# A convolved-attention stage: block-shaped matmuls of a step in one section, transposes, scores and projections in another

## What is computed

```python
    B, T, D = x.shape                       # 8, 256, 256
    hd = D // H                             # 16 heads of 16
    attn = jnp.einsum('bhqd,bhkd->bhqk', q, k) * hd ** (-0.5)
    ...                                     # kernels: 9 taps for each of the B*H maps, from the context
    attn0 = jnp.where(mask, 0.0, attn).reshape(1, B * H, T, T)
    attn = lax.conv_general_dilated(attn0, kernels, window_strides=(1, 1), padding=((1, 1), (1, 1)),
                                    feature_group_count=B * H, ...).reshape(B, H, T, T)
    attn = jnp.where(mask, -jnp.inf, attn)
    p = jax.nn.softmax(attn, axis=-1)
    out = jnp.einsum('bhqk,bhkd->bhqd', p, v)
```

## Time and profile before

| | |
|---|---|
| median of 3 runs | 2229.43 us (2223.65 to 2230.05) |
| the profiled execution | 2223.91 us, span 2222.2 us |
| mean granted clock of TensorE in it | 0.907 |
| the stage's regular part, 632 to 1022 us | 390.0 us, granted clock 1.00 |
| busy in that part: TensorE, ScalarE, VectorE, GpSimd | 337, 206, 204, 200 us |

### The profile page before, as it was taken

The page is one execution under the profiler, slowest core; times in us unless marked ns, Lnnn a source line. Parts: engine busy times, 40 slices in busy tenths (PEclk is TensorE's granted clock), DMA queues, the critical chain, the costliest instruction groups (busy, mean ns, idle before and its releaser), DMA issues. The chain is left out here.

```text
span 2222.2 us, 40660 instructions
## 1 busy us (share of the span) xinstructions
PE 1821.4 (82%) x13563; PEld 1308.2 (59%) x13585; DVE 1031.4 (46%) x3515; ACT 957.6 (43%) x2468; POOL 743.3 (33%) x904
## 2 busy tenths in 40 slices
PE   6849999989598888887499988984893988887594
PEld 5737766666344444444389965644782866555493
DVE  2552224653455555553400058865346546984323
ACT  3633221432345555555333346754442435775220
POOL 1012202110355555542011054410645737641233
PEclk9959999999699999999689999995895998999697
DMA  4313212000311111100289944416676685433394
GB/s 146 115 52 133 64 41 94 19 20 8 54 35 32 34 36 33 34 20 9 84 322 355 332 132 103 114 51 254 197 150 252 183 150 136 108 93 123 98 352 128
DMA packets 171224, 260.81 MB, mean 117 GB/s; under 512 B 23056, under 2 KB 136592, under 8 KB 166928
## 3 DMA queue, kind: packets, MB, share of 16 engines
q1 hardware_dynamic: 150960, 208.65, 28.9%
q0 software_dynamic: 16704, 45.64, 9.3%
q10 hardware_dynamic: 3360, 3.93, 0.7%
HBM read 181.46 MB, written 37.75 MB: 99 GB/s over the span
## 5 line engine op out<-in xcount | busy, mean ns | idle before, releaser
L508 POOL DMA_INDIRECT weights_xg<-xn_rows,token_of x197 | 189.2, 961 | 418.9 <-DVE token_of L698 168.5
L1893 ACT ACTIVATE heads_probsT<-heads_ps_e 128x512 f32<-128x512 f32 x256 | 148.1, 597 | 69.2 <-PE heads_ps_e L1736 62.4
L1047 PE MATMUL experts_ps_g<-weights_w,experts_xT 128*128 x504 | 136.4, 395 | 1.7 <-issue 0.7
L1070 PE MATMUL experts_ps_y<-weights_w,experts_hT 128*128 (+1 forms) x486 | 134.1, 385 | 1.2 <-DVE experts_y L1132 1.2
L2224 PE MATMUL heads_ps_t<-ident,heads_mixes 128*128 128x128 f32 x576 | 103.5, 288 | 32.0 <-ACT heads_probsT L2318 19.5
L2307 ACT ACTIVATE heads_mixes<-heads_mixes,heads_least 128x256 f32<-128x256 f32 x288 | 118.4, 497 | 17.9 <-DVE heads_least L2464 17.9
L1712 PE MATMUL heads_ps_m<-heads_stackK,heads_stackQ 96*128 96x256 bf16 x512 | 100.1, 280 | 23.6 <-DMA heads_stackQ<-heads_q_pieces 9.4
L1104 ACT ACTIVATE experts_silu<-experts_ps_g 128x128 f32<-128x128 f32 (+1 forms) x165 | 53.0, 321 | 153.2 <-PE experts_ps_u L1052 80.3
L2201 PE MATMUL heads_ps_c<-heads_S,heads_band 32*32 32x512 f32 x3072 | 112.8, 606 | 0.4 <-DVE heads_least L2464 0.4
L2318 ACT COPY heads_probsT<-heads_ps_t 128x240 f32<-128x240 f32 x256 | 84.8, 362 | 64.4 <-PE heads_ps_t L2224 62.7
L2224 PEld LDWEIGHTS heads_ps_t<-ident,heads_mixes 128*128 128x128 f32 x576 | 60.1, 141 | 79.3 <-issue 70.1
(11 more groups left out here) (443 smaller groups left out, 4319.3 us busy)
## 6 DMA issues: line engine op xcount, KB each, us to landing
experts_w<-in_experts_dram SPq DMA_DIRECT2D x23, 2180.0 KB, 10.4
weights_w<-in_experts_dram SPq DMA_DIRECT2D x32, 768.0 KB, 5.7
weights_w<-in_experts_dram SPq DMA_DIRECT2D x14, 1536.0 KB, 18.7
y_rows<-experts_y SPq DMA_DIRECT2D x125, 128.0 KB, 1.8
heads_stackK<-heads_k_pieces SPq DMA_DIRECT2D x192, 64.0 KB, 2.6
heads_stackQ<-heads_q_pieces SPq DMA_DIRECT2D x192, 64.0 KB, 3.1
weights_w<-in_experts_dram SPq DMA_DIRECT2D x8, 1088.0 KB, 5.5
xn_rows<-xn SPq DMA_DIRECT2D x4, 2048.0 KB, 7.6
```

The source lines that it names most:

```text
L508: pool.indirect_dma_start(self.xg[:, u, :], None, xn_dram, bass.IndirectOffsetOnAxis(ap=tb.token_of[:, j:j + 1], axis=0)).then_inc(self.x_ ...
L1047: last = pe.matmul(ps_g[:, j % 2, 0:2 * F], xT[:, j % 2, c, :], w[:, bass.ds(at_slot(at[j], c * 2 * F), 2 * F)], start=(c == 0), stop=(c = ...
L1070: last = pe.matmul(ps_y[:, j % BY, 0:D], hT[0:m, j % 2, f * P:(f + 1) * P], w[0:m, bass.ds(at_slot(at[j], DC * 2 * F + f * D), D)], start= ...
L1893: act.activation(probsT[:, h, :], ps_e[:, h % 2, :], ACT.Exp).then_inc(exped, 1)
```

## The change

Nothing that is computed changes, and no instruction is added or removed but waits. The orders on TensorE and VectorE change, with the banks and the semaphore counts that follow from them:

- TensorE's step begins with the three taps of the convolution in a row, then the mix, then score_last of quad n+1. These are all the products that use tiles smaller than the array's full width. Behind them the turns; convolve_last stands behind turn 1, the third score behind turn 3, the fourth behind turn 5, the query and key projection behind turn 5 (it was 2), the value projection behind turn 6 (it was 3). The first two scores, of quad n+2, end the step behind turn_back.
- The scores 0 and 2, score_last and the query projection use bank 0 of ps_s; the scores 1 and 3, convolve_last and the value projection bank 1. The ninth-strip score now comes third of its quad.
- ORDER puts the ninth strip fourth instead of first. VectorE interleaves: drops 0 and 1 of quad n+1, row_max 0 and 1, drop_masked_last, row_max 2 to 4, drop 2, row_max 5 and 6, drop 3, row_max 7 and 8, then finish and take as before.
- ScalarE places the values behind copy 7 (it was 4).

```diff
-    ORDER = (8, 0, 4, 1, 5, 2, 6, 3, 7)
+    ORDER = (0, 4, 1, 8, 5, 2, 6, 3, 7)
+    AT = [ORDER.index(k) for k in range(NW)]
...
             def score(n, j):
-                u, bank = n // 2, (0, 1, 1, 0)[j]
+                u, bank = n // 2, (0, 1, 0, 1)[j]
...
-                if j < 2 and n > 0:
-                    pe.wait_ge(masked, ENTRIES * (n - 1) + GH + j)
-                if j == 0 and n >= 3 and n % 2 == 1:
-                    pe.wait_ge(qk_taken, min((n + 5) // 2, ROUNDS))
-                if j == 1 and n >= 3 and n % 2 == 1:
-                    pe.wait_ge(v_placed, (n + 1) // 2)
+                    if n > 0:
+                        pe.wait_ge(masked, ENTRIES * (n - 1) + 4)
+                    if n >= 3 and n % 2 == 1:
+                        pe.wait_ge(qk_taken, min((n + 5) // 2, ROUNDS))
+                if j == 1:
+                    if n > 0:
+                        pe.wait_ge(masked, ENTRIES * n)
+                    if n >= 3 and n % 2 == 1:
+                        pe.wait_ge(v_placed, (n + 1) // 2)
                 if j == 2:
-                    pe.wait_ge(masked, ENTRIES * n + 2)
+                    pe.wait_ge(masked, ENTRIES * n + 3)
                 if j == 3:
-                    pe.wait_ge(masked, ENTRIES * n + 1)
                     if n > 0:
-                        pe.wait_ge(maxed, NW * (n - 1) + 1)
+                        pe.wait_ge(maxed, NW * (n - 1) + AT[8] + 1)
...
             def score_last(n):
-                pe.wait_ge(masked, ENTRIES * n + 3)
+                pe.wait_ge(masked, ENTRIES * n + 1)
...
             def convolve(n, dk):
                 if dk == 0:
                     pe.wait_ge(band_ready, n + 1)
-                    pe.wait_ge(masked, ENTRIES * n + GH)
+                    pe.wait_ge(masked, ENTRIES * (n + 1))
                 for i in range(GROUPS):
                     if dk == 0 and n > 0:
-                        pe.wait_ge(maxed, NW * (n - 1) + 1 + 2 * (i + 1))
+                        pe.wait_ge(maxed, NW * (n - 1) + AT[i + GROUPS] + 1)
...
             def convolve_last(n):
-                pe.wait_ge(masked, min(ENTRIES * (n + 1) + 1, ENTRIES * QUADS))
+                pe.wait_ge(masked, min(ENTRIES * (n + 1) + 2, ENTRIES * QUADS))
...
             for n in range(QUADS + 2):
                 ahead, back = n + 1 < QUADS, 1 <= n <= QUADS
-                if ahead:
-                    score(n + 1, 0)
-                    score(n + 1, 1)
                 if n < QUADS:
-                    convolve(n, 0)
-                    convolve_last(n)
-                if ahead:
-                    score(n + 1, 2)
-                if n < QUADS:
-                    convolve(n, 1)
-                if ahead:
-                    score(n + 1, 3)
-                    score_last(n + 1)
-                if n < QUADS:
-                    convolve(n, 2)
+                    for dk in range(TAPS):
+                        convolve(n, dk)
                 if n >= 2:
                     mix(n - 2)
+                if ahead:
+                    score_last(n + 1)
                 for k in range(NW):
                     if back:
                         turn(n - 1, k)
-                    if k == 2 and n % 2 == 1 and n // 2 + 3 < ROUNDS:
-                        pe.wait_ge(masked, ENTRIES * (n + 1) + GH)
+                    if k == 1 and n < QUADS:
+                        convolve_last(n)
+                    if k == 3 and ahead:
+                        score(n + 1, 2)
+                    if k == 5 and ahead:
+                        score(n + 1, 3)
+                    if k == 5 and n % 2 == 1 and n // 2 + 3 < ROUNDS:
+                        pe.wait_ge(masked, ENTRIES * (n + 1) + 4)
                         project_query_key(n // 2 + 3, 0)
-                    if k == 3 and n % 2 == 1 and n // 2 + 1 < ROUNDS:
+                    if k == 6 and n % 2 == 1 and n // 2 + 1 < ROUNDS:
                         pe.wait_ge(masked, ENTRIES * (n + 2))
                         project_value(n // 2 + 1, 1)
                 if n >= 2:
                     turn_back(n - 2)
+                if n + 2 < QUADS:
+                    score(n + 2, 0)
+                    score(n + 2, 1)
...
             def row_max(n, k):
                 at = ORDER[k]
-                if k == 0:
+                if k == 0 and n >= 2:
+                    v.wait_ge(turned, NW * (n - 1))
+                if at == NW - 1:
                     v.wait_ge(convolved_last, n + 1)
...
-            for n in range(-1, QUADS + 2):
-                if n + 1 < QUADS:
+            for n in range(QUADS + 2):
+                ahead = n + 1 < QUADS
+                if ahead:
                     drop_masked(n + 1, 0)
                     drop_masked(n + 1, 1)
-                if 0 <= n < QUADS:
-                    row_max(n, 0)
-                if n + 1 < QUADS:
-                    drop_masked(n + 1, 2)
-                    drop_masked(n + 1, 3)
-                    drop_masked_last(n + 1)
-                if 0 <= n < QUADS:
-                    for k in range(1, NW):
+                for k in range(NW):
+                    if n < QUADS:
                         row_max(n, k)
+                    if k == 1 and ahead:
+                        drop_masked_last(n + 1)
+                    if k == 4 and ahead:
+                        drop_masked(n + 1, 2)
+                    if k == 6 and ahead:
+                        drop_masked(n + 1, 3)
                 if n >= 2:
                     finish(n - 2)
```

More of the change, by code:

```diff
@@ L2183, in score_last @@
                 r = u % STACKS
-                pe.wait_ge(masked, ENTRIES * n + 3)
+                pe.wait_ge(masked, ENTRIES * n + 1)
                 for j in range(GH):
                     h = GH * (n % 2) + j
-                    last = pe.matmul(ps_s[LANE * j:LANE * (j + 1), 1, 0:SEQ], stackQ[:, r, h, 2 * P:QW],
+                    last = pe.matmul(ps_s[LANE * j:LANE * (j + 1), 0, 0:SEQ], stackQ[:, r, h, 2 * P:QW],
                                      stackK[:, r, h, :], start=True, stop=True, skip_group_check=True)
@@ L2207, in convolve_last @@
             def convolve_last(n):
-                pe.wait_ge(masked, min(ENTRIES * (n + 1) + 1, ENTRIES * QUADS))
+                pe.wait_ge(masked, min(ENTRIES * (n + 1) + 2, ENTRIES * QUADS))
                 for dk in range(TAPS):
-                    last = pe.matmul(ps_s[:, 0, 0:SEQ], band_last[:, n % 2, dk, :, :].rearrange("p j m -> p (j m)"),
+                    last = pe.matmul(ps_s[:, 1, 0:SEQ], band_last[:, n % 2, dk, :, :].rearrange("p j m -> p (j m)"),
                                      S_last[:, n % 2, dk:dk + SEQ], start=(dk == 0), stop=(dk == TAPS - 1),
@@ L2255, in _ @@
             pe.wait_ge(v_placed, 1)
-            for j in range(GH):
-                score(0, j)
+            score(0, 0)
+            score(0, 1)
             score_last(0)
+            score(0, 2)
+            score(0, 3)
+            score(1, 0)
+            score(1, 1)
             pe.wait_ge(constants, 1)
@@ L2347, in _ @@
                         copy_turned(n - 1, k)
-                    if k == 4 and n % 2 == 1 and n // 2 + 1 < ROUNDS:
+                    if k == 7 and n % 2 == 1 and n // 2 + 1 < ROUNDS:
                         place_values(n // 2 + 1)
@@ L2438, in drop_masked @@
             def drop_masked(n, j):
-                bank = (0, 1, 1, 0)[j]
-                v.wait_ge(scored, ENTRIES * n + j + 1)
+                v.wait_ge(scored, ENTRIES * n + (1, 2, 4, 5)[j])
                 if j == 0 and n >= 2:
@@ L2500, in _ @@
             v.wait_ge(masks_ready, 2)
-            for n in range(-1, QUADS + 2):
-                if n + 1 < QUADS:
+            drop_masked(0, 0)
+            drop_masked(0, 1)
+            drop_masked_last(0)
+            drop_masked(0, 2)
+            drop_masked(0, 3)
+            for n in range(QUADS + 2):
+                ahead = n + 1 < QUADS
+                if ahead:
                     drop_masked(n + 1, 0)
                     drop_masked(n + 1, 1)
-                if 0 <= n < QUADS:
-                    row_max(n, 0)
-                if n + 1 < QUADS:
-                    drop_masked(n + 1, 2)
-                    drop_masked(n + 1, 3)
-                    drop_masked_last(n + 1)
-                if 0 <= n < QUADS:
-                    for k in range(1, NW):
-                        row_max(n, k)
+                for k in range(NW):
+                    if n < QUADS:
+                        row_max(n, k)
+                    if k == 1 and ahead:
[4 more added lines that the diff above has]
+                        drop_masked(n + 1, 3)
                 if n >= 2:
```

14 lines of the change are left out of this document (7 added, 7 removed).

## The result

| | before | after |
|---|---|---|
| median | 2229.74 us (2223.65 to 2231.49, 4 runs) | 2207.85 us (2206.49 to 2209.86, 4 runs) |
| ratio | 1 | 0.9907, 95% interval 0.9887 to 0.9928 |
| the stage, from its first score to the start of its last mix, in the profiled execution | 436.2 us | 415.9 us |
| granted clock in its regular part | 1.00 | 0.96 |

The change makes the kernel 0.9% faster, 21.9 us. The forecast was 33 us. The granted clock is the share of TensorE's full speed that the profile records for a stretch.

The account below looks back on a forecast made before the run. TensorE's own instruction order was taken as the bound. Gains of 18.5, 10.7 and 1.2 made 30 us: 2223.9 to 2194, plus half of 5.5, 2196 us; own range 2186 to 2206, 8 in 10 2182 to 2212.

Parts of the forecast that it names:

- The three taps: Head of TensorE's step: three taps in a row take 3.35 us against 3.21 before, a loss of 0.14.
- Turn 1: Behind the mix on TensorE: still waits for its copy, 1.72 us after the mix starts; score_last runs inside that wait.
- Conv_last: Ninth-strip convolution behind turn 1: 1.30 us instead of 1.40, priced at six of the projection's eight pieces.
- From turn 2 to the turn back: Even step, 6.60 to 9.76: ring rounds of 0.95 us, with scores 2 and 3 covered; uncovered they cost 0.6 a step.
- The even step: TensorE's even step ends at 10.54 us instead of 11.77, a gain of 1.23, or 18.5 us over 15 steps.
- The odd step: TensorE's odd step: 14.70 us against 15.52, a gain of 0.82, with its 2.05 us stall before the scores kept whole.
- VectorE's last row_max: row_max 8 ends at 10.2, before the next convolution's last row group needs it at 10.5: 0.3 us to spare.
- rival (d): Drop 2 or 3 on VectorE comes late and holds the projections: about 9 us gained, 2218 us; chance 0.05.
- (a): Grouping pays by itself: the taps cost 3.0 us together instead of 3.35, 11 us more gained, 2185 us; chance 0.12.
- (b): Nothing is hidden: scores between turns cost their full 0.31 and delay the ring; 3 us gained, 2224 us; chance 0.10.
- (c): VectorE becomes last, the next step's first tap waits and TensorE's clock falls: 3.4 us a step, 2251 us; chance 0.07.
- A granted clock below 1.00 in the regular part: Listed among the signs that would show the forecast wrong; the stage's regular part ran at 1.00 before the change.

Follow-up runs that it names:

- e6: The changed kernel with take ahead of finish on VectorE (no stall), third and fourth scores made twice: 2176.6 us, against 2168.5 us without the doubling.
- e3: The changed kernel with its stall filled by four full-size products whose result is overwritten and not used: 2189.7 us.
- e11: The kernel before with the three taps in a row and take ahead of finish on VectorE, so without the stall: 2222.6 us, ratio 0.9972.
- e8: The kernel before, stall kept, with the third score of each step made twice: 2257.0 us, ratio 1.0136.
- e5: The changed kernel, stall kept, with the ninth-strip convolution moved from behind turn 1 to behind the first tap: 2231.0 us.
- e4: The changed kernel with its stall filled by 16 block-shaped 32x32 tiles whose result is overwritten and not used: 2194.8 us.

## Why the prediction was right, and where it was off

**Held, by its steps.** The three taps: 3.35 forecast, 3.33 measured; that the third would cost 1.08 and not the 1.20 of the second had no row behind it, and came out. Turn 1 at 1.72 behind the mix (763.58 to 765.30), with score_last inside that wait. Conv_last 1.30 (765.54 to 766.84). From turn 2 to the turn back 3.16 forecast, 3.09 measured (766.84 to 769.93), with the scores inside; e6 doubled them and confirmed the cover. The even step 10.54, measured 10.46 where the clock stays up. The odd step 14.70, measured 14.67; its stall was foreseen to stay whole, and is 2.05 (782.80 to 784.85). VectorE's last row_max, the smallest cover named, passed by 0.3. The rows of VectorE, SyncE and GpSimd of the kernel after:

```profile
769.97 0.42 DVE L2471 CUSTOM_DVE_ANT_0 heads_mixes<-heads_ps_c,heads_mask_add 128x256 f32<-128x256 f32 x1
...
768.71 0.55 SPq L2135 DMA_DIRECT2D heads_stackQ<-heads_pieces  x1
...
771.84 1.01 POOL L2385 TENSOR_TENSOR heads_band_last<-heads_band,heads_own_rows 128x384 f32<-128x384 f32 x1
```

It ends at 770.39 and the taps begin at 770.71. The stack's transfers start 10.1 into this step (1.6 of it the slow taps) and the band is done 14.2 into it; neither is waited for.

**The step that failed.** 2207.85 lies outside the forecast's own range, 2186 to 2206, and inside the range of 8 in 10, 2182 to 2212, whose upper part was there for rival (d), late drops. What filled it was something else, so that it was wide enough is luck. The step that failed is the one that was not written as a term: the sum prices every piece of the regular part at clock 1.00, because the earlier trace rows shows 1.00. That price hung on the stalls leaving the clock alone, as they did before, and no reason was given why they would go on doing so in another order. Eight slow tap sections cost 11.3 us, and filling the stall gave 10.8 back (e3). For the stage the forecast was 30 us, measured are 20.3, and 20.3 + 11.3 = 31.6. The forecast of 33 for the median is larger than 30 because it set out from the profiled execution and added only half of the 5.5 us by which the median of before stood above it; the measured median fell by 1.6 more than the stage.

**The rivals.** (a) fell: the taps cost 3.33 in a row, not 3.0, and e11 shows grouping, with the waits that it brings in the old order, as a loss of 20.8 us; the gain is from what moved between the turns. (b) fell with e6. (c) had the place and the symptom right (first tap, clock down, 1.0 to 1.6 us each) and the cause wrong: VectorE was in time, and what lowered the clock stood ahead of the taps, in the stall that the forecast carried over as harmless. (d) fell: no drop held a projection. "A granted clock below 1.00 in the regular part" was named as a sign of being wrong, and it came: the places of the sum held, the clock at which they were priced did not.

**What stays open.** Why one stall lowers the clock and the next, of the same length, doesn't. Seven kernels without idle stalls had no fall in the regular part, five with stalls at changed distances had 5 to 11 in 12, and the kernel before had none in two executions with its stalls 27.3 us apart. An equal distance by itself doesn't spare a stall: those of e8 are as equal, 30.7 us, and each has its fall, and in e5 stalls 27.0 us apart are spared (771.69, 798.71) and then hit (825.76). Theory D puts the difference down to the moment at which a stall comes; that is argued and not shown, since no run set the moment or the distance by itself with all else equal.

## What to carry to other kernels

A granted clock of 1.00 in the profile of before was a property of that timing, not of the order alone (e8): where a loop has a TensorE wait like this one, 1.65 us, price a change with and without a fall of the clock behind it, and look for what would remove the wait, since two exchanged calls on VectorE gave here more (39 us on top) than the reordering itself (22). Grouping work of one shape was not a gain by itself here; what paid was putting independent work where a ring of two buffers left the engine idle. Filling a wait with useless products is a cheap test of whether the clock is what a section has lost.

## What was not expected of the hardware

Behind an idle time of 1.65 us on TensorE the granted clock went to 0.50 (5 to 11 of 12 times in five kernels), while the same 1.65 us left it at 1.00 all 24 times in two executions of the kernel before. 0.22 us more work in an even step of 11.8 us made the kernel 30 us slower; without the stall the same work added 5.7 us to the stage. Block-shaped 32x32 products in the wait (e4) kept the clock at 1.00, as full-size ones did (e3).
